# Cross attention on one core: ctx and x turned by DMA instead of TensorE, projections and score pieces dealt anew, V copied by ScalarE

## The reference, cut to what matters

```python
# B=8 batches, x (8, 224, 512), ctx (8, 750, 512), 16 heads of 32, float32
q = (x @ Wq.T + bq)     # split in heads
k = (ctx @ Wk.T + bk)
v = (ctx @ Wv.T + bv)
att = softmax(q @ k.T / sqrt(32))
out = (att @ v) @ Wo.T + bo + x
out = (out - mean) / sqrt(var + 1e-5) * gamma + beta
```

## Time and profile before

| | |
|---|---|
| median of three runs | 669.68 us |
| the profiled execution's own time | 673.01 us |
| its span, first to last instruction | 670.3 us |
| mean granted clock of TensorE | 0.985 |
| TensorE, VectorE, ScalarE, GpSimd busy | 97%, 71%, 49%, 68% |
| DMA, mean of the 16 engines over the span | 29.2% |

### The profile page before, as it was taken

How to read it: one execution, slowest core, us unless ns; L and a number is a source line. 1 busy time by engine, 2 the same in 40 slices (tenths; PEclk the granted TensorE clock), 3 DMA queues, 4 the chain that set the end, 5 groups by cost and what they waited for, 6 DMA issues and landing times.

```text
span 670.3 us, 15116 instructions
## 1 busy us (share of the span) xinstructions
PE 647.2 (97%) x5441; PEld 448.9 (67%) x5441; DVE 477.8 (71%) x680; ACT 331.4 (49%) x657; POOL 455.2 (68%) x458
## 2 busy tenths in 40 slices
PE   8999999999999999999999999999999999999893
PEld 7757676766776666766767667776667767665452
DVE  4667767778767786777767786677867777667865
ACT  4514645554555554554455545455445544545460
POOL 9303765777957587675957779575877758678942
PEclk9999999999999999999999999999999999999787
DMA  9392412232232232332233322322323201331000
GB/s 289 124 236 71 113 42 73 60 85 74 57 97 71 62 86 75 88 74 84 56 80 88 88 72 58 96 68 66 88 77 90 57 3 35 84 87 32 28 30 28
DMA packets 39562, 53.08 MB, mean 79 GB/s; under 512 B 13436, under 2 KB 25736, under 8 KB 39496
## 3 DMA queue, kind: packets, MB, share of 16 engines
q1 hardware_dynamic: 39496, 52.16, 29.2%
HBM read 24.52 MB, written 3.67 MB: 42 GB/s over the span
## 4 chain that ended last, share of the span: by engine, by line
PE 87%; DVE 5%; POOL 3%; issue 2%; DMA 1%; ACT 1%; SPq 0%; DVEq 0%; POOLq 0%; ACTq 0%
PE ps_task L504 39%; PE ps_scores L515 11%; PE ps_task L555 11%; PE ps_scoresT L539 11%; PE ps_task L467 6%; PE ps_task L477 2%; PE ps_scores L504 2%; PE ps_task L581 2%; DVE top L777 2%; POOL pair_sums L886 2%; PE ps_task L481 1%; PE ps_scoresT L524 1%; DVE y L751 1%; DVE parts L739 1%; DMA ctx_in<-in_ctx 1%
## 5 line engine op out<-in xcount | busy, mean ns | idle before, releaser
L777 DVE TENSOR_REDUCE top<-ps_scores 112x1 f32<-112x750 f32 x256 | 235.7, 928 | 114.1 <-PE ps_scores L515 113.5
L886 POOL TENSOR_TENSOR pair_sums<-probsT 125x672 f32<-125x672 f32 x122 | 198.8, 1629 | 164.7 <-ACT probsT L678 159.4
L678 ACT ACTIVATE probsT<-ps_scoresT 125x448 f32<-125x448 f32 x384 | 188.5, 546 | 121.5 <-PE ps_scoresT L539 118.5
L515 PE MATMUL ps_scores<-stacks 96*112 96x512 f16 (+1 forms) x512 | 126.7, 329 | 5.3 <-DVE top L777 4.1
L504 PE MATMUL ps_task<-wvT,ctxT 128*125 128x512 f16 x564 | 129.9, 380 | 0.7 <-DVE ctxT L741 0.7
L504 PE MATMUL ps_task<-ctxT,wkT 128*128 128x375 f16 x708 | 122.7, 323 | 0.1
L539 PE MATMUL ps_scoresT<-stacks 100*125 100x224 f16 x768 | 116.5, 267 | 1.3 <-ACT probsT L678 0.2
L539 PEld LDWEIGHTS ps_scoresT<-stacks 100*125 100x125 f16 x768 | 83.5, 138 | 32.0 <-ACT probsT L678 12.4
L504 PEld LDWEIGHTS ps_task<-wvT,ctxT 128*125 128x125 f16 x564 | 74.6, 136 | 39.6 <-DVE ctxT L741 0.9
L504 PEld LDWEIGHTS ps_task<-ctxT,wkT 128*128 128x128 f16 x708 | 68.8, 97 | 37.4 <-DVE v L744 0.5
L891 POOL TENSOR_TENSOR head_sums<-pair_sums 125x224 f32<-125x224 f32 x122 | 84.2, 690 | 10.4
(11 more groups left out here) (94 smaller groups left out, 594.3 us busy)
## 6 DMA issues: line engine op xcount, KB each, us to landing
stacks<-parts SPq DMA_DIRECT2D x256, 60.9 KB, 2.0
ctx_in<-in_ctx SPq DMA_DIRECT2D x16, 672.0 KB
stacks<-parts SPq DMA_DIRECT2D x128, 46.9 KB, 2.0
x_in<-in_x SPq DMA_DIRECT2D x8, 448.0 KB, 3.6
resid<-in_x SPq DMA_DIRECT2D x8, 448.0 KB, 3.8
out_y<-y SPq DMA_DIRECT2D x16, 224.0 KB, 2.3
stacks<-parts SPq DMA_DIRECT2D x128, 14.0 KB, 1.8
ctx_in<-in_ctx SPq DMA_DIRECT2D x16, 78.0 KB
```

The costliest lines, as they stand in the source:

```text
L515: last = nc.tensor.matmul(ps_scores[0:QP, s % RING, keys], stacks[0:STACK_ROWS, g, h, NK + QP * q:NK + QP * q + QP], stacks[0:STACK_ROWS, ...
L678: nc.scalar.activation(probsT[0:KP, g % 2, h, 2 * j:2 * j + 2, :].rearrange("p k q -> p (k q)"), ps_scoresT[0:KP, piece % 2, 0:2 * NQ], AC ...
L777: nc.vector.tensor_reduce(top[0:QP, g % 2, HG * q + h:HG * q + h + 1], ps_scores[0:QP, s % RING, 0:NK], AX.X, ALU.max).then_inc(top_ready, 1)
L886: nc.gpsimd.tensor_tensor(pair_sums[0:KP], probsT[0:KP, g % 2, h, 0:3, :], probsT[0:KP, g % 2, h, 3:6, :], ALU.add).then_inc(pair_sums_rea ...
```

## The change

- The six tiles of ctx are now five of 128 rows and one of 110 (`CTX_TILES`), x is 128 and 96 rows. The tasks "ctxT" and "xT" go out of `NEXT`; the prologue still turns batch 0 by TensorE.
- For the next batch ScalarE writes the high part of a tile of tokens, straight from the loaded float32 tile (`token_high`), VectorE the low part (`token_low`), at steps 1, 1, 3, 9, 9, 11 (ctx) and 17, 17 (x), into one of four slots. SP then issues one DMA transpose for the tile, both parts (`turn`), when the last reader of the old ctxT columns is through.
- ctx_in holds three tiles instead of six; the second half of ctx is loaded within the batch, behind the split of ctx 2. In batch 0 it lies in head_sums.
- The projections K, Q, V move into other steps; steps 2, 6, 10, 12, 16, 20, 23 and 30 of a batch hold no task now.
- The pieces are dealt by a table, as (before the task, behind the task) of each step. Batch 7 from step 8 on and the end keep two a step.
- ScalarE copies V out of its bank (at the start of the next step, behind the exps of the step before); VectorE waits for that and counts the task, now behind its row maximum.
- Small tiles (attn, recip) share memory.

```diff
+    EVEN = (((0, 0),) * 2 + ((2, 0),) * 6) * UNITS
+    PIECES_IN = ((0, 0), (0, 0), (1, 0), (2, 0), (2, 0), (2, 1), (1, 0), (2, 1),
+                 (0, 0), (0, 0), (1, 0), (2, 1), (1, 0), (2, 0), (2, 0), (2, 1),
+                 (0, 0), (0, 0), (2, 0), (2, 1), (1, 0), (2, 0), (2, 1), (1, 0),
+                 (0, 0), (0, 0), (2, 0), (2, 0), (2, 0), (2, 1), (1, 0), (2, 0))
     OWN = {0: ("K", 2, 1), 3: ("K", 3, 1), 4: ("Q", 2), 5: ("V", 3), 7: ("V", 4), 8: ("Q", 3), 11: ("V", 5)}
-    NEXT = {2: ("ctxT", 0), 6: ("ctxT", 1), 10: ("ctxT", 2), 12: ("xT", 0), 13: ("K", 0, 0), 14: ("ctxT", 3), 15: ("V", 0),
-            16: ("ctxT", 4), 19: ("K", 1, 0), 20: ("ctxT", 5), 22: ("V", 1), 23: ("xT", 1), 24: ("K", 0, 1), 26: ("Q", 0),
-            27: ("V", 2), 28: ("Q", 1), 29: ("K", 1, 1), 30: ("K", 2, 0), 31: ("K", 3, 0)}
+    NEXT = {13: ("K", 0, 0), 14: ("K", 1, 0), 15: ("V", 0), 19: ("K", 0, 1), 22: ("V", 1), 24: ("Q", 0), 26: ("V", 2),
+            27: ("Q", 1), 28: ("K", 1, 1), 29: ("K", 2, 0), 31: ("K", 3, 0)}
+    SPLIT = {1: (("ctxT", 0), ("ctxT", 1)), 3: (("ctxT", 2),), 9: (("ctxT", 3), ("ctxT", 4)), 11: (("ctxT", 5),),
+             17: (("xT", 0), ("xT", 1))}
+    FIRST_READERS = (("K", 0, 0), ("K", 0, 1), ("Q", 0))
+    LAST_READERS = {("ctxT", 2): ("V", 3), ("ctxT", 3): ("V", 4), ("ctxT", 4): ("V", 5), ("ctxT", 5): ("V", 5),
+                    ("xT", 0): ("Q", 3), ("xT", 1): ("Q", 3)}
...
+            def turn(t):
+                sp.dma_start_transpose(tokens_turned(t),
+                                       token_parts[0:padded_rows(t), split_place(t)[1]].rearrange("p a d -> p (a d)")).then_inc(turned[t], DMA)
...
+                def turn_when_free(t):
+                    sp.wait_ge(task_ready, after(LAST_READERS[t]) if t in LAST_READERS else before)
+                    sp.sem_inc(split_seen, 1)
+                    wait_split(t)
+                    sp.sem_inc(split_seen, 1)
+                    turn(t)
...
+                if has_next(b):
+                    for i in range(2):
+                        turn_when_free(("ctxT", i))
+                    wait_split(("ctxT", 2))
+                    load_ctx(b + 1, 1)
                 if 0 in tasks:
+                    fill(2, ("K", 2, 1), ("Q", 2))
+                if has_next(b):
+                    for i in range(2, CT):
+                        turn_when_free(("ctxT", i))
+                    if more_loads:
+                        load_ctx(b + 2, 0)
+                if 0 in tasks:
+                    fill(3, ("K", 3, 1), ("Q", 3))
+                if has_next(b):
+                    for i in range(2):
+                        turn_when_free(("xT", i))
+                    if more_loads:
+                        load_x(b + 2)
+                    fill(0, ("K", 0, 0), ("K", 0, 1), ("Q", 0))
...
+                if t[0] == "V":
+                    nc.scalar.copy(v[parity][0:KP, t[1]], bank[0:KP, :]).then_inc(v_saved, 1)
+                    return
...
+            def token_high(t, batch):
+                if t[0] == "ctxT":
+                    act.wait_ge(ctx_loaded[t[1] // HALF_TILES], DMA * (1 + t[1] // HALF_TILES) * (batch + 1))
+                else:
+                    act.wait_ge(x_loaded, DMA * len(X_TILES) * (batch + 1))
+                held, back = slot_before(t)
+                need(act, turned[held], DMA * (batch - back))
+                rows_in = slice(0, padded_rows(t))
+                nc.scalar.copy(token_parts[rows_in, split_place(t)[1], 0], tokens_in(t, batch)[rows_in]).then_inc(token_high_saved, 1)
...
+            def token_low(t, batch):
+                dve.wait_ge(token_high_saved, len(SPLIT_ORDER) * (batch - 1) + split_place(t)[0] + 1)
+                rows_in, slot = slice(0, padded_rows(t)), split_place(t)[1]
+                nc.vector.tensor_tensor(token_parts[rows_in, slot, 1], tokens_in(t, batch)[rows_in], token_parts[rows_in, slot, 0],
+                                        ALU.subtract).then_inc(token_low_saved, 1)
```

More of the change, by code:

```diff
@@ L146, in inputs_of, with split_place, slot_before, rows_of @@
     def inputs_of(t):
[L148 to L152, removed]
+        if t[0] == "Q":
+            return [("xT", 0), ("xT", 1)]
+        first, n = (KP * t[1], KP) if t[0] == "V" else (KH * t[2], KH)
+        return [("ctxT", i) for i in range(first // P, (first + n - 1) // P + 1)]
+    def split_place(t):
+        return SPLIT_ORDER.index(t), SPLIT_ORDER.index(t) % SPLIT_SLOTS
+    def slot_before(t):
+        n, slot = split_place(t)
+        same = [i for i in range(len(SPLIT_ORDER)) if i % SPLIT_SLOTS == slot]
+        at = same.index(n)
+        return (SPLIT_ORDER[same[at - 1]], 0) if at else (SPLIT_ORDER[same[-1]], 1)
+    def rows_of(t):
+        tokens = (CTX_TILES if t[0] == "ctxT" else X_TILES)[t[1]]
+        return tokens.stop - tokens.start
     def batch_of(t, s, b):
@@ L320, in visit_before, with pieces_of @@
             return unit_before(b, at // UNIT, 2) if at >= 0 and at % UNIT == VISIT else None
-        def pieces_of(s):
-            i = s % UNIT
-            return (2 * i - 4, 2 * i - 3) if i >= 2 else ()
+        def pieces_of(b, s, behind):
+            table = EVEN if isinstance(b, int) and (b == B or b == LAST and s >= UNIT) else PIECES_IN
+            slot = s - s % UNIT
+            first = sum(sum(n) for n in table[slot:s]) + (table[s][0] if behind else 0)
+            return range(first, first + table[s][behind])
         def split_views(t, bank, part):
             kind = t[0]
[L330 to L335, removed]
+            if kind in ("ctxT", "xT"):
+                tokens, of = (CTX_TILES, ctxT) if kind == "ctxT" else (X_TILES, xT)
+                n = rows_of(t)
+                return of[:, part, :, tokens[t[1]]], bank[:, 0:DT * n].rearrange("p (k t) -> p k t", k=DT), None
             if kind == "W":
@@ L395, in _ @@
             fill_stack(0)
-            for half in range(2):
-                load_ctx(1, half)
+            load_ctx(1, 0)
             load_x(1)
@@ L630, in iteration @@
                         t, place, _ = tasks[s]
-                        pe.wait_ge(task_saved, before + max([saved_by(b, s - TASK_BANKS) if not (isinstance(b, int) and b == B) else 0] + [tasks[STEP_OF[i]][1] + 1 for i in inputs_of(t)]))
+                        pe.wait_ge(task_saved, before + (saved_by(b, s - TASK_BANKS) if not (isinstance(b, int) and b == B) else 0))
+                        if t in FIRST_READERS:
+                            for i in inputs_of(t):
+                                pe.wait_ge(turned[i], DMA * batch_of(t, s, b))
                         visited = visit_before(b, s)
@@ L720, in iteration @@
                         attn_high(u, g_u, after_o)
+                    u = unit_before(b, g, 1)
+                    if u is not None:
+                        for piece in pieces_of(b, s, True):
+                            exp(u, (g - 1) % UNITS, piece)
             batches(act, iteration)
@@ L826, in iteration @@
                     saved = to_save(b, s)
-                    if saved is not None and saved[0][0] == "V":
-                        t, n, splits, bank, batch, of_next = saved
-                        save_task(t, n, splits, bank, batch, 1 - parity if of_next and s else parity)
                     if has_step(b, s + 1):
@@ L833, in iteration @@
                         mean_of(O_STEPS.index(s - 2))
[L834 removed]
+                    if saved is not None:
                         t, n, splits, bank, batch, of_next = saved
[L836 removed]
+                        v_copied = None if t[0] != "V" else v_copies(b, s)
+                        save_task(t, n, splits, bank, batch, parity, v_copied)
                     for back, i, h in SUM_STEPS:
```

141 lines of the change are left out of this document (84 added, 57 removed).

## The result

| | before | after |
|---|---|---|
| median of 4 runs each on one chip, us | 670.88 | 685.35 (684.09 to 689.86) |
| ratio, 95% interval | | 1.0223 (1.0188 to 1.0258) |
| profiled execution, its span | 673.01, 670.3 | 684.09, 682.0 |
| mean granted clock in it | 0.985 | 0.985 |

Slower, by 14.5 us, more than twice the 6.3 that was forecast, still inside the range of 659 to 700. A later comparison gave 685.13 against 671.02, 1.0213 (1.0169 to 1.0257).

What follows compares the result with a forecast made beforehand. TensorE bounds the kernel, with exps setting its pace: 72.77 of work plus 5.86 of waits makes 78.6 a batch for 77.83. +4.8 for six batches, +2.5 late ctx 2, -0.5 end: 676 us, own range 669 to 684, overall 659 to 700.

Steps and rivals of the forecast that it cites:

- the term for GpSimd's sums: At step 25 the visit comes 0.3 earlier but GpSimd's last sum no earlier, so sum_keys waits 0.3 to 0.4 us.
- late ctx 2: In batch 0, ctx 2's turn queues behind stack 2 on SP, so K(0,0) waits once, 2 to 3 us, taken 2.5.
- 20/21: Step 20: O(1) still begins 2.34 after the projection's end, so the removed turn's 0.43 becomes wait: 0.94 us.
- 30/31: Step 30: exp behind the copy, then K(3,0) needs VectorE's low part of K(2,0), behind a maximum: 0.84 us.
- The exps as the pace: Where turns go, the chain of piece, exp and bank sets TensorE's pace; waits at eight places, 5.48 us a batch.
- V's copy on ScalarE: ScalarE's V copy, about 594 ns, delays the next exp: 0.72 us each at steps 6 and 12.
- The rival of late sums: New low parts block GpSimd's sums in steps 9, 17 and 1: +1.3 us a batch, 685 us; chance 0.12.
- The base: One middle batch of the kernel before, 77.83 us, against which the forecast batch of 78.6 gave +0.8.
- The turn: One 256 KB DMA per tile on SP's queue: 1.5 us to issue, 2.0 to 5.1 until landed.
- The rival of the SP queue: A turn holding SP over 3 us makes its queue the bound: 705 to 730 us; chance 0.18, with a late turn.
- The low parts: VectorE's eight 512-column low parts of tokens from SBUF, taken at 0.8 us each; no engine bound.
- The end: The end keeps its even deal; in batch 7 VectorE is rid of three copies: -0.5 us.

Runs made afterwards that it cites:

- e1: Changed kernel with the even deal, two pieces in each of a unit's steps 2 to 7, in all batches: 676.34 us, ratio 1.0051.
- e3: Kernel before, with only one of four TensorE transposes in each ctx and x turn in the loop (output not the reference's): 670.37 us, ratio 0.9941.
- e2: Changed kernel with V copied by VectorE ahead of its row maximum again: 683.2 us, ratio 1.0137.
- e6: Changed kernel with x's two splits at step 18 instead of 17: 682.72 us, ratio 1.0160.
- e5: Changed kernel with ctx 2 turned ahead of stack 2's 16 DMAs on SP: 682.7 us, ratio 1.0133.
- e4: Changed kernel without tokens' loads, splits and DMA turns for batches 1 to 7, all computing on batch 0's tokens: 676.42 us, ratio 1.0062.
- e10: The e8 kernel with the changed kernel's own table of deals back for batches 0 to 6: 670.07 us, ratio 0.9991.
- e11: The e8 kernel with V copied by ScalarE and counted by VectorE behind its maximum, as in the changed kernel: 674.02 us, ratio 1.0044.
- e8: Changed kernel with V on VectorE, ctx 2 first, x split at 18, earlier K saves, later O(1) statistics and a new deal table: 665.84 us, ratio 0.9901.

## Why the prediction was right in kind and wrong in size

The step that failed is the term for GpSimd's sums: 0.35 a batch with nothing at step 17, measured 1.30. The price of the late ctx 2 in batch 0 was the second, 2.5 for 4.7. Both mechanisms had been seen; what stood behind them had not been followed.

The ten waits of a batch, worked out start to start as in the prediction (time between two tasks less 0.19 for each piece and 0.32 for each scores):

| steps | forecast | measured |
|---|---|---|
| 2/3, 10/11 behind visits | 0.49, 0.57 | 0.34, 0.35 |
| 6/7, 12/13 behind V's copy | 0.72, 0.72 | 0.75, 0.87 |
| 20/21 | 0.94 | 0.95 |
| 30/31 | 0.84 | 0.82 |
| visit of 17, Q(0) of 24 for V | 0.60, 0.60 | 0.44, 0.33 |
| sum_keys of 17 | 0 | 0.66 |
| sum_keys of 25 | 0.35 | 0.64 |
| sum | 5.86 (rounded) | 6.15 |

- *The exps as the pace:* right, shown by e1 and e3 and by the eight terms, 4.85 measured for 5.48. Work without waits, 72.77, and 6.15 give 78.92; the batch took 78.88.
- *V's copy on ScalarE:* 581 ns for 594, and a price of four waits. Right in the changed kernel's rows. That its removal alone would give little (e2) followed from the sums, which I had not chained behind the visit.
- *GpSimd's sums:* this step failed. I counted 0.35 at step 25, on the premise that the sums come no earlier, and nothing at step 17. The sums came later: the new table puts a unit's last piece behind V(0), so the last exp ahead of the visit of step 17 ends 0.62 before it instead of 2.63, and the visit of step 25 has 1.27 instead of 2.26. Measured are 0.66 (of which e6, the split's share, gave back about 0.3) and 0.64, together 1.30, without a loss at step 1. The even deal (e1) leaves 0 and 0.37, which is the forecast's term. The two are +0.95 over the forecast, the eight others -0.63.
- *The rival of late sums* had 1.3 a batch too, but laid it to the splits in steps 9, 17 and 1; it was the deal first, and steps 17 and 25. That its 685 is the measured median is luck: 1.3 for 0.35 in six batches on 676.5 gives 682, and the rest is batch 0 and the clock.
- *The base:* I set 78.6 against one batch of 77.83. Batches 5 and 6 of the kernel before take 77.46 each and those of the changed one 78.88 and 78.74; over five periods the difference is 1.32 where 0.8 stood. And the period with the loop's jump, which I had not looked at, took another 0.8 more than that in this trace.
- *The late ctx 2:* right as an event (a turn issued at 62.82, forecast by 63.5; wait 2.86), wrong as a price: 2.5 was the wait alone. Behind it the granted clock was 0.64, and the start came 4.7 later. e5 took back 4.4 by turning one tile earlier.
- *The turn:* an issue of 1.4 to 1.6 us from start to start and 3.2 to 3.4 to landing; 1.5 and 2.0 to 5.1 forecast, and not the 10.5 of the rival's last estimate. e4 showed that steady batches don't feel it. The rival of the SP queue falls.
- *The low parts:* 1100 ns on the mean (0.8 taken). No engine was bound by them.
- *The end:* -1.1 for -0.5 in this trace; the changed kernel's other one is 3.0 shorter there, so this term can't be told from none.

Forecast +6.8 on the profiled execution, +11.7 in its span: of the missing 5, 2.2 are batch 0 (mostly its clock), 3.4 the batches and the loop (1.32 x 5 + 1.6 - 4.8), and the end gave 0.6 back. The rest, up to the medians' 14, goes with the lower clock of most runs.

The loop's period is 4.0 to 4.3 us longer than its neighbours in e1, e5, e10, e11 and the changed kernel's other trace, and 1.7 to 2.5 in the nine others. The granted clock of the 4 us behind the jump divides them in the same way: 0.57 to 0.61 in those five, 1.00 in the nine. Open: what decides whether it falls. The idle time before it doesn't tell, since it was 1.95 in e11, where the clock fell, and 2.24 in e8, where it didn't.

## What to carry to other kernels

Work on the bounding engine is worth its length only if nothing it stands between is in step with another engine. Here 3.36 us of transposes a batch covered the latency of piece, exp and bank; without them, and with V's copy in the exp's way, TensorE waited longer than the transposes had taken. So before work is taken off a full engine, measure start to start across it, drop part of it as a trial (e3), and deal the rest anew for the engine that sets the step; for a wait that goes, price what is late next, and for a wait of 2 to 3 us in TensorE's stream, price the clock behind it too. Where work moves, follow it into the engines behind the one that sets the step: here a piece moved behind a copy made an exp late, the exp a sum, and the sum TensorE. And trace one kernel twice before a difference of 2 us in one stretch is laid to an edit.

## What the runs showed of the hardware

- A DMA transpose within SBUF of 128 rows by 1024 float16 columns (256 KB) took 1.26 us to issue on SP's queue (the median of the 42 of ctx in the changed kernel; 1.4 to 1.6 from start to start where two follow one another) and had landed 3.4 (ctx) and 3.2 (x) after its issue, the medians.
- A split of 512 float32 columns from SBUF took VectorE 0.68 us in e8 at a time when GpSimd was free, and 0.87 to 1.75 beside it in the same batch; GpSimd's sum of 224 columns took 0.98 for 0.66:

```profile
423.04 0.68 DVE L871 TENSOR_TENSOR token_parts<-ctx_in,token_parts 128x512 f16<-128x512 f32 x1
```

- The granted clock fell behind an idle time of TensorE of 2.9 us in the changed kernel (0.64 from 66 to 70), behind 1.95 to 2.3 us at the loop's jump in five traces (0.57 to 0.61 in the 4 us after it), and behind 3.6 us in e2, where the wait ended at 68.50: there it was 0.50 for four whole us, the lower of the levels, 1.2 GHz. The stretches of e2:

```profile
66.00:70.00 4.00, 1.50 (x5) 0.72 (x6) 0.00 (x0) 0.00 (x0) 1.92 (x3) 0.71 0.95 183
70.00:74.00 4.00, 4.00 (x16) 2.47 (x15) 0.92 (x2) 1.12 (x3) 0.00 (x0) 0.50 0.79 183
```
